# A graph network kernel: the gathers of the message stages in a POOL loop, their indices copied six at a time, and the sums of PE in a loop

## The chip, the cores and the metric

The kernel runs on one core of a Trainium2 chip. The metric is the device time of one execution in microseconds (us). The engines are TensorE (PE, its weight loads PEld), VectorE (DVE), ScalarE (ACT), GpSimd (POOL) and SyncE (SP); DMA engines move data between device memory and the on-chip memory (SBUF). Engines wait for each other with semaphores, all written out by hand.

## The reference

Four graph layers run over the same graph: 625 nodes of 768 features and 10000 edges (src, dst, a type of 8 and a type of 34), each on relu(layernorm(x)) and added to x. The layers that matter here are the relational ones. Cut to that:

```python
def _rgcn_conv(x, src, dst, etype, W, root, b):
    seg = dst * num_rel + etype
    sums = segment_sum(x[src], seg)
    cnt = segment_sum(ones, seg)
    mean = (sums / maximum(cnt, 1.0)).reshape(num_nodes, num_rel, -1)
    return einsum('nri,rio->no', mean, W) + x @ root + b
# layer 0: two of these (8 types, relu between); layer 1: one (34 types), then a GCN; layers 2 and 3: graph attention
```

## The kernel before

For a relational layer the kernel multiplies first and sums along the edges afterwards. PE makes h·W_r for every type r, each float32 product as three passes of high and low parts (line 1553), ACT takes the results out of PSUM, and SP stores them as the rows of a table `U` in device memory. Then comes a *message stage*, three in all: phase 0 and 1 for the two convolutions with 8 types, phase 2 for the one with 34.

The edges were sorted by groups of 128 destination nodes and cut into NT = 84 tiles of 128 edges. For each tile four things happen in a message stage:

- POOL issues an indirect DMA (`gathers`, line 473) that brings the tile's 128 rows of `U`, 393 KB, into one of GB = 6 buffers `gat`. Before it, it waits for `agg_pe`: tile t needs tile t-6 to have been summed.
- DVE makes the tile's one-hot matrix with the edge weights (line 944), four buffers deep, waiting for the same `agg_pe`.
- PE waits for the one-hot and the gather and runs two float32 matmuls of 512 and 256 columns (line 1461; four records in a trace), which add the tile to the sums of its group in PSUM; the second raises `agg_pe`. Which PSUM bank it is comes from a register: every six tiles PE loads a packed number `grp` (line 1423).
- Nothing else of weight runs then: ACT is idle, and SP's loads for the next phase wait for buffers.

So the order is a ring: gather, DMA, PE, release, gather, with six buffers in it. POOL's gathers and PE's tiles are written out 84 times each per phase; the row numbers of a gather are read straight from the table `ix[:, table, t]`. DVE's part is a loop of seven turns of twelve tiles (GU = 12).

Elsewhere POOL already works in loops: `kinv` (lines 478 to 484) and `lookup` copy six columns of `ix` into a small tile `ixb` at a register's offset (`indices`, line 464), wait for the copy with `pool_idx`, and use `ixb` in six indirect DMAs. `indices` counts the semaphore `pool_idx` by a number k of earlier whole tables. The instruction `pool.sem_inc(S["pool_nop"], 1)` carries the wait that stands before it, since a DMA whose wait needs a register has it in front of it.

Of the kernel before, what the change touches and what calls it, by code (L numbers as in the profile page):

```python
# [24 lines left out]
NP = NG * P  # L25
# [4 lines left out]
NT = 84  # L30
R0, R1 = 8, 34
# [7 lines left out]
GB = 6  # L39
MB = 4  # L40
GU = 2 * GB
# [5 lines left out]
def gnn_kernel(nc, a, out):  # L47
    ctx = ExitStack()
    with ctx:
        def sb(name, shape, dt=F32):  # L50
            return ctx.enter_context(nc.sbuf_tensor(name, shape, dt))

        def sem(name):
            return ctx.enter_context(nc.semaphore(name))
# [12 lines left out]
        gat = arena[:, 6528:6528 + GB * D].rearrange("p (b n) -> p b n", b=GB)  # L67
# [40 lines left out]
        def edge(shape, dt=F32):  # L108
# [39 lines left out]
        ix = sb("ix", [P, 4, NT], I32)  # L148
        ixb = sb("ixb", [P, GU], I32)
# [38 lines left out]
        U = nc.dram_tensor("U", [R1 * NP, D], F32, kind="Internal").ap()  # L188
# [8 lines left out]
        S = {n: sem(n) for n in (  # L197
            "x_in edges_in dve_nop w64_in consts vec_ok ln_var ln_std ln_h hT_tp hT_hi hT_lo "
            "w_hi w_lo steps evac pool_idx pool_nop msg_oh agg_pe acc_out "
            "srt_rs srt_ps srt_rhs srt_mm srt_tab cnt_oh cnt_pe k_inv kinv_st w_pr w_done "  # L200
            "key_ok key_tp ov_ok urow_st urow_ok u_zero l_oh l_pe l_ix h_st lix_ok hc_tp hc_hi hc_lo "
            "v_in v_hi v_lo v_mm v_ev "
            "c_oh c_pe ct_tp ct_cp deg_ok deg_sq gcn_y gcn_mm gcn_ev x_ok ln_c ln_cc ct_ln "
            "elu_v elu_m elu_e bd_z bd_tp bd_ok ft_mm ft_ev chain out_st").split()}
# [7 lines left out]
        g_in = [sem(f"g_in{b}") for b in range(GB)]  # L212
# [51 lines left out]
        def sums(c0, g=None):  # L264
            if g is None:
                return ps[:, 0:NG, :] if c0 == 0 else psf[:, 512 * NG:512 * NG + 256 * NG].rearrange("p (g n) -> p g n", g=NG)
            return psf[:, ds(512 * g, 512)] if c0 == 0 else psf[:, ds(512 * NG + 256 * g, 256)]
# [172 lines left out]
        def _(pool):  # L440
# [21 lines left out]
            def indices(table, it, j, k):  # L462

                pool.tensor_copy(ixb[:, j:j + GB], ix[:, table, ds(GU * it + j, GB)]).then_inc(S["pool_idx"], 1)  # L464
                pool.wait_ge(S["pool_idx"], NT // GB * k + 2 * it + j // GB + 1)
                pool.sem_inc(S["pool_nop"], 1)

            def gathers(phase):

                table = (0, 0, 3)[phase]  # L470
                for t in range(NT):
                    pool.wait_ge(S["agg_pe"], NT * phase + t + 1)
                    pool.indirect_dma_start(out=gat[:, t % GB, :], out_offset=None, in_=U[0:NP * (R0, R0, R1)[phase], :],  # L473
                                            in_offset=bass.IndirectOffsetOnAxis(ap=ix[:, table, t:t + 1], axis=0)).then_inc(g_in[t % GB], 16)

            pool.wait_ge(S["srt_tab"], 1)
            pool.wait_ge(S["kinv_st"], 16)
            with pool.Fori(0, NT // GU) as it:
                for j in range(GU):
                    if j % GB == 0:  # L480
# [3 lines left out]
                                            in_offset=bass.IndirectOffsetOnAxis(ap=ixb[:, j:j + 1], axis=0)).then_inc(k_in[j // GB], 16)  # L484
            pool.wait_ge(S["w_done"], NT // GB + 2)
            for g in range(NG):
                pool.wait_ge(u_st[g], 16 * (ST_C1 + 2 * R0))
            gathers(0)

            pool.wait_ge(S["urow_st"], 16)  # L490
            def urow_out(it, j):

                pool.wait_ge(k_in[j], 16 * GB * it + 16 * GB * (NT // GU + 1))
                pool.tensor_copy(ix[:, 3, ds(GU * it + GB * j, GB)], urow_g[:, GB * j:GB * (j + 1)]).then_inc(S["urow_ok"], 1)

            def lookup(it, first):
                for j in range(2):
                    indices(1, it, GB * j, 1)
                    if not (first and j == 0):
                        pool.wait_ge(S["urow_ok"], 2 * it + j - 1 + 1)  # L500
                        pool.sem_inc(S["pool_nop"], 1)
                    for k in range(GB * j, GB * (j + 1)):
                        pool.indirect_dma_start(out=urow_g[:, k:k + 1], out_offset=None, in_=urow_d,
                                                in_offset=bass.IndirectOffsetOnAxis(ap=ixb[:, k:k + 1], axis=0)).then_inc(k_in[j], 16)
                    if j == 1:
                        urow_out(it, 0)
                    elif not first:
                        urow_out(it - 1, 1)
            pool.sem_inc(S["urow_ok"], 1)
            lookup(0, True)  # L510
            with pool.Fori(1, NT // GU) as it:
                lookup(it, False)
# [3 lines left out]
            for g in range(NG):  # L516
                pool.wait_ge(u_st[g], 16 * (ST_C2 + 2 * R0))
            gathers(1)

            pool.wait_ge(S["l_ix"], 1)  # L520
            pool.wait_ge(S["h_st"], 16)
            pool.wait_ge(S["hT_tp"], 3 * KT)
            with pool.Fori(0, R1 // 2) as it:
                for j in range(2):
# [4 lines left out]
                    for g in range(TC):  # L529
                        pool.indirect_dma_start(out=src_rows[:, TC * j + g, :], out_offset=None, in_=h_d,  # L530
                                                in_offset=bass.IndirectOffsetOnAxis(ap=lixb[:, j, g:g + 1], axis=0)).then_inc(hc_in[j], 16)
# [11 lines left out]
            for j in range(2):  # L543
                pool.wait_ge(v_st[j], n_ov * 16 + 16)
                pool.sem_inc(S["pool_nop"], 1)
            gathers(2)


# [848 lines left out]
        def _(pe):  # L1397
# [22 lines left out]
            def group(it, stride, o):  # L1420

                if o % GB == 0:
                    packed[0] = pe.value_load(grp[0:1, ds(stride // GB * it + o // GB, 1)], min_val=0, max_val=8 ** GB - 1)
                return ((packed[0] >> (3 * (o % GB))) & 7).with_bounds(min_val=0, max_val=NG - 1)
# [4 lines left out]
            def clear(i, banks):  # L1429

                if i:
                    pe.wait_ge(S["acc_out"], i)
                else:
                    pe.wait_ge(S["k_inv"], 1)
                for b in banks:
                    pe.matmul(ps[:, b, :], z16[:, 0:P], z16[:], start=True, stop=True)
# [13 lines left out]
            def messages(ph, q, i):  # L1450

                pe.wait_ge(S["evac"], 5 * q + 2)
                clear(i, range(8))
                for it in range(NT // GU):
                    for o in range(GU):
                        b = o % MB
                        g = group(it, GU, o)
                        pe.wait_ge(S["msg_oh"], NT * ph + o + GU * it + 1)
                        pe.wait_ge(g_in[o % GB], 16 * (NT // GB * ph + 2 * it + o // GB + 1))
                        for c0, c1 in ((0, 512), (512, D)):  # L1460
                            ins = pe.matmul(sums(c0, g), onehot[:, b, :], gat[:, o % GB, c0:c1], start=False,  # L1461
                                            stop=True, skip_group_check=True)
                        ins.then_inc(S["agg_pe"], 1)
# [176 lines left out]
            pe.wait_ge(S["hT_lo"], KT)  # L1640
            phase(Q_C1, R0)
            messages(0, Q_C2, 0)
            pe.wait_ge(S["acc_out"], 1)
            transpose(1)
            pe.wait_ge(S["hT_lo"], 2 * KT)
            clear(1, range(2, 8))
            phase(Q_C2, R0, 18, c_side(0))
            pe.wait_ge(S["l_ix"], 1)
            messages(1, Q_L1, 2)
            pe.wait_ge(S["ln_h"], 2 * NG)  # L1650
            transpose(2)
            pe.wait_ge(S["hT_lo"], 3 * KT)
            clear(3, range(2, 2 + NG))
            relations(6, c_side(1))
            further()
            messages(2, Q_GCN, 4)
            pe.wait_ge(S["acc_out"], 5)

            for s in range(NG):
                if s >= 2:  # L1660
                    pe.wait_ge(S["ct_cp"], s - 1)
                b = 4 + 2 * (s % 2)
# [10 lines left out]
            for i in range(2 * NG):  # L1673
                j, cols = i // 2, slice((i % 2) * HALF, (i % 2 + 1) * HALF)
# [72 lines left out]
            for g in range(NG):  # L1747
                b = 4 + 2 * (g % 2)
# [47 lines left out]
```

## Time and profile before

| | us |
|---|---|
| median of 3 runs | 2478.19 (2472.67 to 2482.26) |
| the profiled execution | 2472.67, its span 2470.9 |
| the three message stages, first to last matmul (392.67 to 512.55, 918.77 to 1039.81, 1689.39 to 1816.84) | 119.9, 121.0, 127.5 |
| busy in the span: PE / DVE / ACT / POOL | 2081.0 / 1192.3 / 696.7 / 567.3 |
| granted TensorE clock, mean | 0.883 |

The page gives busy time by engine, then the chain of work that ended last, then the costliest groups of instructions with the idle time before them. A timeline row reads: start, duration, engine, line, operation, and in brackets the idle time of that engine before it and what ended it. "issue" means that nothing in the profile ended it.

### The profile page before, as it was taken

The page shows a single profiled execution, that of the slowest core. Times are in us where ns is not written, and L with a number is a line of the kernel's source. Part 1 is how long each engine was busy: PE and PEld are TensorE (multiplying, and loading weights), DVE is VectorE, ACT ScalarE, POOL GpSimd, SP SyncE. Part 2 cuts the span into 40 slices and gives each one's busy share as a digit, 9 for nine tenths or more (in the row PEclk, how much of TensorE's full clock was granted, in tenths as well). Part 3 has the DMA queues.
Part 4 walks back from the last instruction along what each step waited for, and adds up shares of the span by engine and source line. Part 5 has one row for each costly group of instructions (what it writes and reads, how often), then busy time and mean ns, then how long its engine had stood idle before and what let it go on. Part 6 is the DMA issues. An engine that isn't in the chain of part 4 may idle for free.

```text
span 2470.9 us, 34116 instructions
## 1 busy us (share of the span) xinstructions
PE 2081.0 (84%) x10546; PEld 1774.8 (72%) x10547; DVE 1192.3 (48%) x2113; ACT 696.7 (28%) x899; POOL 567.3 (23%) x586
## 2 busy tenths in 40 slices
PE   3999879989998799779999999967988666667885
PEld 3999776567788785479999989954565656537775
DVE  5741213243342362345555555442233689546995
ACT  1222210012222110024545444530020256113553
POOL 0001765610006736412222222104620000000000
PEclk9999999989999899989999999978999766775555
DMA  3456547834445238637887777757830022001221
GB/s 108 152 172 181 160 120 245 272 95 142 141 151 176 90 120 265 213 123 241 264 264 254 260 249 259 246 185 239 272 121 7 18 81 89 12 24 44 65 64 53
DMA packets 206670, 385.13 MB, mean 156 GB/s; under 512 B 19347, under 2 KB 174373, under 8 KB 206590
## 3 DMA queue, kind: packets, MB, share of 16 engines
q1 hardware_dynamic: 173934, 253.16, 31.5%
q0 software_dynamic: 31216, 128.89, 16.9%
q10 hardware_dynamic: 1440, 1.97, 0.2%
q8 instruction: 55, 0.90, 0.1%
q14 instruction: 25, 0.20, 0.0%
HBM read 295.56 MB, written 88.39 MB: 155 GB/s over the span
## 4 chain that ended last, share of the span: by engine, by line
PE 65%; DVE 15%; issue 8%; DMA 6%; ACT 2%; another core or an unknown queue 2%; DVEq 1%; POOL 0%; SPq 0%; ACTq 0%; POOLq 0%
PE ps L1553 41%; PE ps L1461 12%; DVE arena L1244 2%; DMA arena<-U,ix 2%; DMA arena<-in_L_gnn_W_rel 2%; DVE arena L1267 2%; PE ps L1566 2%; DVE arena L1275 1%; PE ps L1753 1%; PE ps L1679 1%; PE ps L1720 1%; PE ps L1447 1%; PE ps L1406 1%; PE ps L1445 1%
## 5 line engine op out<-in xcount | busy, mean ns | idle before, releaser
L1553 PE MATMUL ps<-w_hi,hT_hi 128*128 128x384 f32 x2172 | 772.0, 355 | 62.9 <-DVE hT_lo L991 20.1
L1553 PE MATMUL ps<-w_hi,hT_lo 128*128 128x384 f32 x2172 | 744.1, 343 | 0.7 <-issue 0.6
L1553 PE MATMUL ps<-w_lo,hT_hi 128*128 128x384 f32 x2172 | 743.8, 342 | 1.0 <-issue 1.0
L1553 PEld LDWEIGHTS ps<-w_hi,hT_hi 128*128 128x128 f32 x2172 | 423.1, 195 | 76.2 <-issue 33.6
L1553 PEld LDWEIGHTS ps<-w_lo,hT_hi 128*128 128x128 f32 x2172 | 422.5, 195 | 2.6 <-issue 2.2
L1553 PEld LDWEIGHTS ps<-w_hi,hT_lo 128*128 128x128 f32 x2172 | 420.9, 194 | 1.2 <-issue 1.1
L1461 PE MATMUL ps<-arena,onehot 128*128 128x512 f32 x1008 | 345.4, 496 | 27.6 <-DMA arena<-U,ix 12.7
L1461 PEld LDWEIGHTS ps<-arena,onehot 128*128 128x128 f32 x1008 | 186.5, 191 | 187.1 <-issue 177.0
L473 POOL DMA_INDIRECT arena<-U,ix x252 | 250.0, 992 | 193.3 <-PE ps L1461 85.7
L1720 PE MATMUL ps<-R,arena 128*128 (+2 forms) x1000 | 211.6, 394 | 62.4 <-ACT arena L732 62.1
L1720 PEld LDWEIGHTS ps<-R,arena 128*128 128x128 f32 x1000 | 202.0, 306 | 78.7 <-issue 75.9
L1019 DVE TENSOR_TENSOR w_lo<-arena,w_hi 128x2304 fp32r<-128x2304 f32 x67 | 171.5, 2560 | 144.3 <-ACT w_hi L615 140.5
L564 ACT ACTIVATE arena<-ps 128x384 f32<-128x384 f32 x160 | 78.3, 492 | 520.8 <-PE ps L1553 410.5
L944 DVE TENSOR_SCALAR onehot<-iota,tab,wgt 128x128 f32<-128x128 f32 x252 | 87.9, 365 | 268.8 <-PE ps L1461 200.8
L827 DVE TENSOR_TENSOR w_lo<-arena,w_hi 128x2304 fp32r<-128x2304 f32 x45 | 114.8, 2554 | 129.8 <-ACT w_hi L557 116.0
L615 ACT ACTIVATE w_hi<-arena 128x2304 fp32r<-128x2304 f32 x67 | 142.6, 2129 | 60.3 <-DMA arena<-in_L_gnn_W_rel 60.2
L526 POOL COPY lixb<-lidx 128x2 int32 x34 | 35.2, 1034 | 388.5 <-PE ps L1566 356.1
L620 ACT ACTIVATE arena<-ps 128x384 f32<-128x384 f32 x136 | 66.5, 489 | 199.9 <-PE ps L1553 186.5
L464 POOL COPY ixb<-ix 128x6 int32 (+1 forms) x28 | 10.5, 374 | 474.6 <-DMA urow_d<-counts 239.7
L1406 PE MATMUL ps<-ident,h 128*128 128x128 f32 x210 | 45.2, 388 | 85.7 <-DVE h L811 60.0
L991 DVE SCALAR_TENSOR_TENSOR hT_lo<-ps,hT_hi 128x512 fp32r<-128x512 f32 x102 | 70.1, 687 | 97.4 <-ACT hT_hi L597 97.4
L1406 PEld LDWEIGHTS ps<-ident,h 128*128 128x128 f32 x210 | 35.9, 201 | 94.7 <-DVE h L811 32.1
(226 smaller groups left out, 2161.5 us busy)
## 6 DMA issues: line engine op xcount, KB each, us to landing
arena<-in_L_gnn_W_rel SPq DMA_DIRECT2D x74, 1152.0 KB, 5.8
U<-arena SPq DMA_DIRECT2D x292, 192.0 KB
arena<-in_L_gnn_W SPq DMA_DIRECT2D x36, 1152.0 KB
U<-z SPq DMA_DIRECT2D x28, 864.0 KB
arena<-terms_d SPq DMA_DIRECT2D x42, 320.0 KB, 3.9
arena<-rows_d SPq DMA_DIRECT2D x21, 320.0 KB, 3.6
arena<-in_L_gnn_root SPq DMA_DIRECT2D x4, 1152.0 KB
arena<-U,ix POOLq DMA_INDIRECT x252
```

Of the source, the lines that this page charges most:

```text
L473: pool.indirect_dma_start(out=gat[:, t % GB, :], out_offset=None, in_=U[0:NP * (R0, R0, R1)[phase], :], in_offset=bass.IndirectOffsetOnAxi ...
L564: act.activation(dst, ps[:, (o + g) % 2, 0:HALF] if len(dst.shape) == 2 else ps[:, (o + g) % 2, 0:HALF].rearrange("p (h c) -> p h c", h=ds ...
L615: act.activation(w_hi[:, 1 - j], raw[:, 1 - j], cp).then_inc(S["w_hi"], 1)
L620: act.activation(ust[:, TC * j + g, :], ps[:, g, 0:HALF], cp).then_inc(S["evac"], 1)
L827: dve.tensor_tensor(w_lo[:, o % 2], raw[:, o % 2], w_hi[:, o % 2].bitcast(F32), ALU.subtract).then_inc(S["w_lo"], 1)
L944: dve.tensor_scalar(onehot[:, b, :], iota[:, 1:P + 1], tab[:, 1, ds(t, 1)], wgt[:, ph // 2, ds(t, 1)], ALU.is_equal, ALU.mult).then_inc(S[ ...
L991: dve.scalar_tensor_tensor(hc[j][1][:, 2 * i:2 * i + 2, :], ps[:, 7, :].rearrange("p (k n) -> p k n", k=2), 0.0, hc[j][0][:, 2 * i:2 * i + ...
L1019: dve.tensor_tensor(w_lo[:, 1 - j], raw[:, 1 - j], w_hi[:, 1 - j].bitcast(F32), ALU.subtract).then_inc(S["w_lo"], 1)
L1406: ins = pe.transpose(psf[:, 512 * b + P * g:512 * b + P * (g + 1)], h[:, g, P * kt:P * (kt + 1)], ident[:])
L1461: ins = pe.matmul(sums(c0, g), onehot[:, b, :], gat[:, o % GB, c0:c1], start=False, stop=True, skip_group_check=True)
L1553: ins = pe.matmul(acc, l, r[:, j, kt, :], start=(n == 0), stop=(n == 3 * KT - 1))
L1720: ins = pe.matmul(ps[:, 6 + j, (c + 1) * g:(c + 1) * (g + 1)], pt[:, b, P * g:P * (g + 1)], R[:, t, ds((2 * it + j) * (c + 1), c + 1)], st ...
```

## The change

POOL's 84 gathers of a phase become a loop of seven turns with twelve gathers. At the first of every six it calls `indices`, so it waits for `agg_pe`, copies six columns of the table to `ixb`, waits for the copy and then issues the DMA; at the other five the wait stands in a semaphore instruction in front of the DMA. PE's message loop turns from written-out code into a loop of seven turns with the same twelve tiles. The numbers k in `indices` move on by one, as there are more copies.

```diff
+            def gather(it, j, phase):
+
+                t = j + GU * it
+                b = j % GB
+                table = (0, 0, 3)[phase]
+                pool.wait_ge(S["agg_pe"], NT * phase + t + 1)
+                if b == 0:
+                    indices(table, it, j, (1, 3, 4)[phase])
+                else:
+                    pool.sem_inc(S["pool_nop"], 1)
+                pool.indirect_dma_start(out=gat[:, b, :], out_offset=None, in_=U[0:NP * (R0, R0, R1)[phase], :],
+                                        in_offset=bass.IndirectOffsetOnAxis(ap=ixb[:, j:j + 1], axis=0)).then_inc(g_in[b], 16)
+
             def gathers(phase):
-
-                table = (0, 0, 3)[phase]
-                for t in range(NT):
-                    pool.wait_ge(S["agg_pe"], NT * phase + t + 1)
-                    pool.indirect_dma_start(out=gat[:, t % GB, :], out_offset=None, in_=U[0:NP * (R0, R0, R1)[phase], :],
-                                            in_offset=bass.IndirectOffsetOnAxis(ap=ix[:, table, t:t + 1], axis=0)).then_inc(g_in[t % GB], 16)
+                with pool.Fori(0, NT // GU) as it:
+                    for j in range(GU):
+                        gather(it, j, phase)
...
-                    indices(1, it, GB * j, 1)
+                    indices(1, it, GB * j, 2)
...
                 clear(i, range(8))
-                for it in range(NT // GU):
+                with pe.Fori(0, NT // GU) as it:
                     for o in range(GU):
```

POOL's queue at phase 0, before; `agg_pe` is the release by PE:

```order
L473 DMA arena<-U,ix 128x768 [waits u_st3,u_st2,u_st4,u_st1,agg_pe,u_st0,w_done]
L473 DMA arena<-U,ix 128x768 [waits agg_pe] x83
```

The same place after the change, the first of seven turns down to the second copy (four of the six gathers' rows read alike):

```order
L482 ISA
L464 ISA [waits agg_pe]
L464 COPY ixb<-ix 128x6
L465 ISA
L478 DMA arena<-U,ixb 128x768 [waits pool_idx]
L473 REGISTER_ALU
L478 DMA arena<-U,ixb 128x768 [waits agg_pe]
...
L464 ISA [waits agg_pe]
L464 COPY ixb<-ix 128x6
L465 REGISTER_ALU
L478 DMA arena<-U,ixb 128x768 [waits pool_idx]
```

Each sixth gather now stands behind a copy that itself waits for PE's release, and each of the others has a register instruction in front.

PE's queue at the seventh tile of phase 0, before:

```order
L1423 TENSOR_LOAD grp
L1423 ISA x2
L1461 REGISTER_ALU [waits g_in0,msg_oh]
L1461 ISA
L1461 MATMUL ps<-arena,onehot 128x512
L1461 ISA
L1461 MATMUL ps<-arena,onehot 128x256
```

And after, the seventh tile and the end of a turn:

```order
L1434 ISA
L1434 TENSOR_LOAD grp
L1434 ISA x2
L1469 REGISTER_ALU
L1470 ISA [waits msg_oh]
L1472 REGISTER_ALU [waits g_in0]
L1472 ISA
L1472 MATMUL ps<-arena,onehot 128x512
L1472 ISA
L1472 MATMUL ps<-arena,onehot 128x256
...
L1465 REGISTER_ALU
L1465 COMPARE_AND_BRANCH
```

PE's matmuls are the same; in front of them the sequencer has one or two register instructions more per tile, one for the address of `grp`, and a branch per twelve tiles.

## Rows read from the trace of the kernel before

**Rows 1.** The page, chain that ended last; costliest groups (the last number: idle before, releaser).
```profile
PE ps L1553 41%; PE ps L1461 12%; DVE arena L1244 2%; DMA arena<-U,ix 2%; DMA arena<-in_L_gnn_W_rel 2%; DVE arena L1267 2%; PE ps L1566 2%; DVE arena L1275 1%; PE ps L1753 1%; PE ps L1679 1%; PE ps L1720 1%; PE ps L1447 1%; PE ps L1406 1%; PE ps L1445 1%
...
L1461 PE MATMUL ps<-arena,onehot 128*128 128x512 f32 x1008 | 345.4, 496 | 27.6 <-DMA arena<-U,ix 12.7
...
L473 POOL DMA_INDIRECT arena<-U,ix x252 | 250.0, 992 | 193.3 <-PE ps L1461 85.7
```

**Rows 2.** Busy time by engine in the three message stages.
```profile
core 0: us, PE busy (x) PEld busy (x) DVE busy (x) ACT busy (x) POOL busy (x), PEclk, DMA share, GB/s
392.60:512.60 120.00, 114.23 (x336) 61.64 (x336) 28.97 (x84) 0.00 (x0) 73.93 (x78) 1.00 0.78 256
918.70:1039.90 121.20, 113.66 (x336) 61.66 (x336) 28.93 (x84) 0.00 (x0) 74.08 (x78) 1.00 0.78 254
1689.30:1816.90 127.60, 117.50 (x336) 63.19 (x336) 28.51 (x84) 0.00 (x0) 77.42 (x82) 0.97 0.79 263
```

**Rows 3.** Timeline of POOL, first message stage: start us, us, instruction, idle before it.
```profile
394.50 0.94 POOL L473 DMA_INDIRECT arena<-U,ix  x1 [11.86 <-PE ps L1461]
395.79 0.94 POOL L473 DMA_INDIRECT arena<-U,ix  x1 [0.34 <-PE ps L1461]
...
406.08 0.94 POOL L473 DMA_INDIRECT arena<-U,ix  x1 [1.61 <-PE ps L1461]
...
442.49 0.95 POOL L473 DMA_INDIRECT arena<-U,ix  x1 [1.80 <-PE ps L1461]
443.74 0.95 POOL L473 DMA_INDIRECT arena<-U,ix  x1 [0.30 <-issue]
...
505.69 0.94 POOL L473 DMA_INDIRECT arena<-U,ix  x1 [1.36 <-PE ps L1461]
```

**Rows 4.** The same of the second and third stage.
```profile
920.60 0.95 POOL L473 DMA_INDIRECT arena<-U,ix  x1 [5.22 <-PE ps L1461]
...
1032.08 0.95 POOL L473 DMA_INDIRECT arena<-U,ix  x1 [0.30 <-issue]
...
1700.51 0.95 POOL L473 DMA_INDIRECT arena<-U,ix  x1 [4.54 <-PE ps L1461]
...
1808.48 0.95 POOL L473 DMA_INDIRECT arena<-U,ix  x1 [0.30 <-issue]
```

**Rows 5.** Timeline of DVE at the pause of 442 us.
```profile
442.41 1.07 DVE L944 TENSOR_SCALAR onehot<-iota,tab,wgt 128x128 f32<-128x128 f32 x3 [2.55 <-PE ps L1461]
```

**Rows 6.** Timeline of PE at the same place.
```profile
439.62 6.72 PE L1461 MATMUL ps<-arena,onehot 128*128 128x512 f32 x20
446.85 1.55 PE L1461 MATMUL ps<-arena,onehot 128*128 128x512 f32 x4 [0.51 <-issue]
448.78 5.42 PE L1461 MATMUL ps<-arena,onehot 128*128 128x512 f32 x16 [0.38 <-DMA arena<-U,ix]
```

**Rows 7.** Timeline of POOL in the loop that gathers the reciprocals.
```profile
302.87 0.97 POOL L483 DMA_INDIRECT counts<-kinv_d,ixb  x1 [0.79 <-issue]
...
309.15 0.95 POOL L483 DMA_INDIRECT counts<-kinv_d,ixb  x1 [0.30 <-issue]
310.09 0.21 POOL L464 COPY ixb<-ix 128x6 int32 x1
311.09 0.97 POOL L483 DMA_INDIRECT counts<-kinv_d,ixb  x1 [0.79 <-POOL ixb L464]
```

**Rows 8.** PE instructions of the loop head L1493 (PEldq: the sequencer): ns min/median/max.
```profile
L1493 PEldq COMPARE_BRANCH  x4: 76/208/212, 569.2 to 696.4; - x4
```

**Rows 9.** The load of the packed groups, L1423.
```profile
L1423 PEldq TENSOR_LOAD <-grp x84: 295/302/905, 161.6 to 1805.6; - x84
```

**Rows 10.** Queues in the first message stage: packets, MB, share.
```profile
q8 instruction: 5, 0.08, 0.3%
```

**Rows 11.** The same in a stretch where PE loops four times.
```profile
q8 instruction: 2, 0.03, 0.1%
```

**Rows 12.** Timeline of PE at the start of the third stage.
```profile
1697.32 2.92 PE L1461 MATMUL ps<-arena,onehot 128*128 128x512 f32 x4 [3.39 <-DMA arena<-U,ix]
```
## The prediction

> **What bounds the kernel now.** I read the page first. Its chain of waits [rows 1] is mostly PE at the weight products (L1553, 41%), which the change leaves alone. The lines that it touches are L1461, the sums of the message stages (12% of the chain), with gathers (arena<-U,ix) for 2% more, and L473, POOL's gathers. So only three stretches matter, 119.9, 121.0 and 127.5 us long, 368.4 together; what the change is worth is read there.
>
> The table by stretch [rows 2] shows PE busy for 114, 114 and 118 us of these: PE is the busiest, but not closed up. POOL is busy only about 74 us in each, which is misleading, because of the 0.30 us between any two gathers. The timeline of POOL gives the real price: 442.49 to 443.74, 1.25 us per gather back to back [rows 3]. PE takes 1.29 per tile while nothing holds it (POOL in step with PE, 394.50 to 395.79 [rows 3]). POOL can hence run only 3% faster than PE. The mean is neither: 77 gathers from 394.50 to 505.69 are 1.444 us each [rows 3], the second stage has 1.448 (77 from 920.60 to 1032.08), the third 1.440 (75 from 1700.51 to 1808.48) [rows 4]. I take 1.444.
>
> Where do the missing 0.15 us per tile go? I followed one pause. POOL sits idle for 1.80 us before its gather at 442.49 and names PE [rows 3]. DVE, which waits for the same semaphore, then starts three one-hots in a row at 442.41 [rows 5]. But PE shows an unbroken run of 20 matmuls from 439.62 to 446.34 [rows 6], five tiles, one end per 1.29 us. So the releases of three tiles arrived together and the oldest came about 2 x 1.29 = 2.6 us late. PE then pays: the gather of 442.49 feeds the tile that starts at 446.85 (4.36 us later), after 0.51 of idle time, and the next tile waits 0.38 more [rows 6]. The first stage has eleven POOL pauses above 1 us after its first gather, in nine places (two of them are double), from 406.08 with 1.61 to 505.69 with 1.36 [rows 3].
>
> The ring explains that. One turn of a buffer is gather to PE 4.36, the tile 1.55 [rows 6], release to gather about 0.3 (the reading of 394.50 to 395.79, where idle is 0.34 [rows 3]), so 6.2 us against six tiles at 1.29 = 7.74. It holds 1.5 us of lateness; 2.6 is 1.1 too much, near the 0.89 that PE is seen idle.
>
> The Trainium skill (Perfetto Trace Analysis, Tensor Engine Instruction) says that a matmul's end in a profile is estimated, and that the semaphore goes up only when PSUM has acknowledged the bytes. This trace agrees: three tiles released together beside evenly spaced ends. By it lateness belongs to PE's writes, and a slower POOL wouldn't cure it.
>
> **The change, part by part.**
>
> *The copy of six indices.* The trace has the new pattern already, in the loop for the reciprocals: last DMA of six at 309.15, copy at 310.09 for 0.21, then 0.79 idle, then the next DMA at 311.09. From 302.87 to 311.09 six DMAs take 8.22 us [rows 7] where six written out take 7.50. So POOL's floor becomes 8.22 / 6 = 1.37 per gather, above PE's 1.29: PE is no longer what sets the pace when nothing is late, POOL is. If nothing else counted, the copy would add 0.12 per gather to a POOL-bound stage. But the stage isn't bound by POOL now: its waits beyond 0.30 come to 111.19 - 77 x 1.25 = 14.9 us per stage, and 13 copies (the first is ahead of PE) add 13 x 0.72 = 9.4, less than that. So much of the cost falls in pauses.
>
> *The wait in front of the DMA.* Where the wait stood on the DMA itself, the DMA began 0.34 after its predecessor though it was waiting for PE [rows 3]. Now a semaphore instruction waits, and the DMA is handed over after it. The nearest rows are the 0.79 from the copy's end to the DMA, across just such an instruction [rows 7]. While POOL is behind, this overlaps the DMA before; only after a pause is it open, 0.79 - 0.3 = 0.5 us. Low bound zero.
>
> *The sum per gather.* Per pause, the new turn is 4.36 + 1.55 + 2.6 + (0.3 or 0.79) = 8.8 or 9.3 us against six gathers in 8.22: 0.6 or 1.1 us too long. Nine places per stage over 77 gathers make 0.070 or 0.129. So the mean becomes 1.37 + 0.07 = 1.44 or 1.37 + 0.13 = 1.50. The two ends are the whole spread of the dispatch cost; I take the middle, 1.47, since each group's first gather pays the copy and the others only the wait. That is +0.026 over 1.444, times 252 = +6.6 us.
>
> *PE's loop.* A taken branch is 0.208 us in PE's sequencer [rows 8], about 0.4 with the register instructions beside it by my estimate (twice the branch), and the load of `grp`, 0.302 [rows 9], gets an address instruction. At 21 turns the worst is 21 x 0.4 = 8.4 us. Most of it lies under the idle time of PE at a group's first tile, since POOL's copy falls in the same tile (8.22 - 7.74 = 0.48 per six). I count a third, +2.5. The saving in PE's code is nothing: five instruction blocks are fetched in the stage, 0.3% of the queues [rows 10].
>
> *The start of a stage.* In the first two, POOL has its first six gathers out 11.86 and 5.22 us before PE frees a buffer [rows 3, 4], so the first copy is hidden. In the third, PE stands 3.39 us for a gather at 1697.32 [rows 12]; the first copy moves that by the copy and its gap, 0.21 + 0.79 = +1.0.
>
> *`lookup` with another k*: the same instructions, 0.
>
> Sum: 6.6 + 2.5 + 1.0 = +10 us. Against the profiled execution, 2472.67, that is 2483; it is the fastest of three runs, 5.5 under the median, so on the median of 2478.19 I predict 2488.
>
> **The rivals.**
>
> *Nothing visible.* The copies fall entirely in POOL's pauses. For it: 14.9 us of pauses per stage against 9.4 of copies. Against: the pauses are not spread like the copies, and after each POOL is behind and runs back to back, where every 0.72 delays a tile. Gives 2478, within 3.
>
> *Faster, the lateness absorbed.* POOL's slower pace widens the ring from 7.74 to 8.22, so it holds 8.22 - 6.2 = 2.0 us of lateness instead of 1.5. If releases come less late when PE has small rests, and stay under 2.0, there are no stalls, and the mean is the floor, 1.37: (1.37 - 1.444) x 252 = -19, with the start -18: 2460. It decides at a lateness of 2.0 us; the one that I read is 2.6, which speaks against.
>
> *Much slower, nothing absorbed.* POOL pauses as long as today and the costs come on top: 0.12 for the copies and 9 x 0.5 / 77 = 0.06 for the waits, 0.18 x 252 = +45, 2523. For it: if each pause is set by lateness counted from POOL's own pace. Against: the ring's sum above.
>
> *Instruction fetches at each turn.* The Trainium skill (Runtime: NRT & Kernel Launch, Instruction fetch mechanics) warns that a taken branch out of the loaded window stalls for a fetch and that unrolled code is preferred. The trace shows no such thing for PE's loops: from 527 to 697 us, with four turns of a longer body, there are two blocks of instructions [rows 11], against five in the stage written out [rows 10], and the longest branch is 0.21 [rows 8]. As a mechanism of this kernel, a turn that waited for one transfer would lose up to what a gather takes to reach PE, 4.36: 21 x 4.36 = +92. I leave it 2%.
>
> **How the numbers follow.** Forecast (slower by 3 to 20 us) 0.55; nothing visible 0.20; lateness absorbed 0.10; nothing absorbed 0.13; fetches 0.02. A measurement of this kernel tells about 0.5%, 12.4 us, from no change. Of the forecast's 0.55, its own range is 2479 to 2500 and about half lies over 2490.6; with 0.15 from the slow rivals that makes slower 0.42. Faster is the absorbed case, 0.10. The rest, 0.48, is no change. The range leaves out the two far slow cases (0.15) and half of the fast one (0.05): 2467 to 2508.
>
> **What would show it.** In the changed profile: POOL's timeline with a copy before every sixth gather and 8.2 us from one to the next in undisturbed places; waits of POOL for PE shorter in total than the 14.9 us per stage above the gaps; mean of gathers 1.45 to 1.50; PE's idle time at L1461 over the 27.6 us of now [rows 1], named by the gather; all of the difference inside the three message stages. It would be wrong if the mean stays at 1.44 or falls towards 1.37 (lateness absorbed), if pauses of POOL keep their 1.2 to 1.9 us and the mean goes over 1.6, or if PE is idle at the loop's turns with nothing named.

## The result, and the profile after

The changed kernel takes 2498.1 us (median of five runs, 2491.17 to 2499.43) against 2481.14 for the kernel before, five runs beside it: ratio 1.008, 95% interval 1.0052 to 1.0108. It is 17 us slower, where 10 us were forecast: under 1%, but the interval leaves out 1. The profiled execution took 2495.63, its span 2493.9.

The page, the chain and the two groups, the lines that answer to [rows 1]:

```profile
PE ps L1564 38%; PE ps L1472 9%; DMA arena<-U,ixb 3%; DMA arena<-in_L_gnn_W_rel 3%; DVE arena L1255 2%; DVE arena L1278 2%; DVE arena L1286 1%; PE ps L1577 1%; PE ps L1764 1%; PE ps L1690 1%; PE ps L1731 1%; PE ps L1458 1%; PE ps L1456 1%; PE ps L1779 1%
...
L1472 PE MATMUL ps<-arena,onehot 128*128 128x512 f32 x1008 | 352.2, 499 | 40.7 <-issue 18.3
...
L478 POOL DMA_INDIRECT arena<-U,ixb x252 | 244.1, 969 | 136.1 <-issue 69.1
```

PE's idle time ahead of the message matmuls went from 27.6 to 40.7 us. POOL's ahead of its gathers fell from 193.3 to 136.1, but that isn't all less waiting: 53 us of the 193.3 were the three waits for a stage to begin, and these now stand ahead of a copy. What names PE fell from 85.7 us [rows 1] to 53.8 ahead of gathers and 18.0 ahead of copies, 71.8 in all. So POOL waits somewhat less, PE more. The three stages by engine, as [rows 2]:

```profile
core 0: us, PE busy (x) PEld busy (x) DVE busy (x) ACT busy (x) POOL busy (x), PEclk, DMA share, GB/s
393.45:521.10 127.65, 116.36 (x336) 60.47 (x336) 29.45 (x82) 0.00 (x0) 77.03 (x91) 1.00 0.75 240
935.85:1064.25 128.40, 115.70 (x336) 61.11 (x336) 28.75 (x82) 0.00 (x0) 76.86 (x91) 1.00 0.74 239
1709.20:1841.24 132.04, 120.16 (x336) 61.92 (x336) 28.43 (x82) 0.00 (x0) 79.98 (x95) 0.97 0.78 253
```

The stages are 7.7, 7.4 and 4.6 us longer, 19.7 together, at the same granted clock. The span is 23.0 longer; the other 3.3 are +0.8 ahead of the first stage, +8.5 between first and second, -4.6 between second and third and -1.4 behind, nearly all in code that the change leaves alone. So the difference is where the forecast had it, and the stages alone grew by twice its size. POOL's timeline in the first stage, as [rows 3]:

```profile
429.25 0.95 POOL L478 DMA_INDIRECT arena<-U,ixb  x1 [1.88 <-PE ps L1472]
431.82 0.96 POOL L478 DMA_INDIRECT arena<-U,ixb  x1 [1.62 <-PE ps L1472]
432.78 0.19 POOL L464 COPY ixb<-ix 128x6 int32 x1
433.80 0.97 POOL L478 DMA_INDIRECT arena<-U,ixb  x1 [0.83 <-issue]
435.08 0.95 POOL L478 DMA_INDIRECT arena<-U,ixb  x1 [0.31 <-issue]
...
440.09 0.95 POOL L478 DMA_INDIRECT arena<-U,ixb  x1 [0.30 <-issue]
441.04 0.20 POOL L464 COPY ixb<-ix 128x6 int32 x1
442.06 0.97 POOL L478 DMA_INDIRECT arena<-U,ixb  x1 [0.82 <-POOL ixb L464]
```

From 433.80 to 442.06 are six gathers and a copy in 8.26 us, the 8.22 of the forecast [rows 7]. But just before them, at 429.25 and 431.82, POOL sits through 1.88 and 1.62 us of waits for PE: the pauses are still there. The mean gather, from the ninth to the last of each stage, is 1.526, 1.547 and 1.550 us, against 1.448, 1.452 and 1.440 in the same measure before; 1.50 was the upper end of the forecast.

The queue of instruction fetches in the first stage, as [rows 10]:

```profile
q8 instruction: 1, 0.02, 0.1%
```

One block instead of five. That is all that the shorter program saves there.

### The profile page after: what moved, and what is told of

The parts are those of the page before. It is cut to its first block, busy times and chain, and to the rows that moved or that the text cites. A ratio compares the mean times of both kernels' runs of the same rounds, so it can differ in the third digit from the quotient of the medians.

```text
span 2493.9 us, 35129 instructions
## 1 busy us (share of the span) xinstructions
PE 2077.0 (83%) x10546; PEld 1758.0 (70%) x10547; DVE 1192.5 (48%) x2113; ACT 695.6 (28%) x899; POOL 574.5 (23%) x628
## 3 DMA queue, kind: packets, MB, share of 16 engines
q10 hardware_dynamic: 1440, 1.97, 0.2%
## 4 chain that ended last, share of the span: by engine, by line
PE 59%; DVE 15%; issue 10%; DMA 8%; another core or an unknown queue 3%; ACT 3%; POOL 1%; DVEq 1%; SPq 0%; POOLq 0%; ACTq 0%
PE ps L1564 38%; PE ps L1472 9%; DMA arena<-U,ixb 3%; DMA arena<-in_L_gnn_W_rel 3%; DVE arena L1255 2%; DVE arena L1278 2%; DVE arena L1286 1%; PE ps L1577 1%; PE ps L1764 1%; PE ps L1690 1%; PE ps L1731 1%; PE ps L1458 1%; PE ps L1456 1%; PE ps L1779 1%
## 5 line engine op out<-in xcount | busy, mean ns | idle before, releaser
L1472 PE MATMUL ps<-arena,onehot 128*128 128x512 f32 x1008 | 352.2, 499 | 40.7 <-issue 18.3
L478 POOL DMA_INDIRECT arena<-U,ixb x252 | 244.1, 969 | 136.1 <-issue 69.1
L464 POOL COPY ixb<-ix 128x6 int32 (+1 forms) x70 | 22.2, 317 | 555.9 <-DMA urow_d<-counts 238.2
L743 ACT ACTIVATE arena<-arena 128x640 f32<-128x640 f32 x100 | 73.4, 734 | 108.0 <-DVE arena L1286 93.2
```

The costliest lines, as they stand in the source:

```text
L478: pool.indirect_dma_start(out=gat[:, b, :], out_offset=None, in_=U[0:NP * (R0, R0, R1)[phase], :], in_offset=bass.IndirectOffsetOnAxis(ap= ...
L743: act.activation(out_tile(i % 2, i % NG), zt[:, i % NG, :], ACT.Exp).then_inc(s["p_ok"], 1)
```

## The experiments

Twelve runs were made, in three groups; each group had one chip and its own runs of the kernel before. These took 2481.9 us (29 runs) in the first, 2421.5 (17) in the second and 2419.4 (23) in the third: the chips differ by 60 us, and this turned out to be a clue. Ratios are to the kernel before of the same group, with 95% intervals. "Mean gather" is measured as above; "stages" is the sum of the three message stages of the one profiled execution. A cost in us in the text is a difference of medians; the ratio is worked out by itself and can differ from it by some us.

| kernel | median us | ratio | stages us | mean gather us |
|---|---|---|---|---|
| **first group** (before 2481.9) | | | | |
| before, profile shown ahead | | | 368.4 | 1.448 / 1.452 / 1.440 |
| PE's loop alone | 2482.31 | 0.9998 (0.9978 to 1.0017) | 366.9 | 1.452 / 1.456 / 1.446 |
| POOL's side alone | 2499.13 | 1.0071 (1.0049 to 1.0093) | 387.7 | 1.519 / 1.533 / 1.530 |
| copies alone | 2491.58 | 1.0052 (1.0032 to 1.0072) | 381.7 | 1.506 / 1.491 / 1.479 |
| wait apart alone | 2488.78 | 1.0039 (1.0017 to 1.0060) | 380.9 | 1.487 / 1.512 / 1.513 |
| **second group** (before 2421.5) | | | | |
| ring of five | 2447.65 | 1.0124 (1.0098 to 1.0150) | 363.6 | 1.425 / 1.377 / 1.387 |
| ring of seven | 2414.19 | 0.9966 (0.9951 to 0.9982) | 333.4 | 1.291 / 1.279 / 1.331 |
| POOL's side written out | 2447.42 | 1.0108 (1.0093 to 1.0123) | 366.0 | 1.407 / 1.405 / 1.468 |
| the same, ring of seven | 2437.66 | 1.0073 (1.0058 to 1.0089) | 357.1 | 1.383 / 1.379 / 1.442 |
| **third group** (before 2419.4) | | | | |
| before again | 2422.22, one run | | 339.7 | 1.297 / 1.320 / 1.295 |
| changed kernel again | 2442.37 | 1.0095 (1.0072 to 1.0118) | 360.4 | 1.391 / 1.402 / 1.412 |
| copies three gathers ahead | 2419.77 | 1.0000 (0.9981 to 1.0019) | 337.4 | 1.299 / 1.304 / 1.312 |
| ring of seven again | 2413.09 | 0.9977 (0.9965 to 0.9990) | 334.8 | 1.291 / 1.283 / 1.334 |

### First group: which part costs

**PE's loop alone.**

```diff
-                for it in range(NT // GU):
+                with pe.Fori(0, NT // GU) as it:
```

> The kernel before with PE's message loop alone turned into a loop of seven turns; POOL's gathers stay written out. Theory A (the sequencer of PE stands at a turn of the loop, as the changed kernel's trace shows it at 426 us: load of grp 0.69, assert 0.69, register instruction 0.70): PE is idle at the first tiles of six for some 10 us more than before in the three stages, and the time goes up by 6 to 12 us. Theory B (PE's loop is free, POOL's side carries the whole difference of 17 to 20 us): within 2 us of before.

Ratio 0.9998. The loop costs nothing that five rounds can tell, although each of its 21 turns has the branch (instructions of the loop head in this kernel, PEldq being PE's sequencer; ns min/median/max):

```profile
L1454 PEldq COMPARE_BRANCH  x21: 3/208/218, 404.2 to 1825.3; - x21
```

In this trace the first matmul behind a turn starts 1.16 us or more (median 1.28) after the end of the branch: PE's sequencer runs about one tile ahead of its matmuls, and 0.208 us of branch fits in.

**POOL's side alone**: the changed kernel with PE's tiles written out as before.

> The kernel before with POOL's side of the change alone (the loop, the copies of six indices, the wait in a semaphore instruction); PE's tiles stay written out. Theory A: 8 to 12 us slower than before, about half of the difference, with a mean of 1.48 us per gather. Theory B: 17 to 20 us slower, 1.53 us per gather. If the two halves hide behind each other, this run and the one with PE's loop add up to more than the difference.

Ratio 1.0071, +17.2 us, inside the interval of the whole change: POOL's side is the whole difference.

**Copies alone.** The 84 gathers stay written out, the wait stays on the DMA itself at five of six:

```diff
                     pool.wait_ge(S["agg_pe"], NT * phase + t + 1)
+                    if t % GB == 0:
+                        indices(table, t // GU, t % GU, (1, 3, 4)[phase])
...
-                                            in_offset=bass.IndirectOffsetOnAxis(ap=ix[:, table, t:t + 1], axis=0)).then_inc(g_in[t % GB], 16)
+                                            in_offset=bass.IndirectOffsetOnAxis(ap=ixb[:, t % GU:t % GU + 1], axis=0)).then_inc(g_in[t % GB], 16)
```

> POOL's gathers written out as before, but the indices copied six at a time as in the change; the wait for PE stays on the DMA itself at the other five. Shows the copy's cost alone: 13 copies per stage of 0.72 us. If the pauses of POOL take most of them in, +2 us in all; by the sum of my prediction's lower end (1.37 + 0.07 per gather) 0 to +2 as well; if nothing is absorbed, 0.12 x 252 = +28 us. I expect +6, less than the whole loop on POOL.

**Wait apart alone.** No copies, indices read from `ix` as before:

```diff
                     pool.wait_ge(S["agg_pe"], NT * phase + t + 1)
+                    pool.sem_inc(S["pool_nop"], 1)
                     pool.indirect_dma_start(...)
```

> POOL's gathers written out and reading the whole table, as before, but the wait for PE stands in a semaphore instruction in front of each DMA. Shows the cost of the hand-over after the wait alone. By my prediction 0.49 us per pause, in a ring of 7.74 us, nine places per stage: 27 x 0.49 = +13 us at most; zero if the sequencer hides it. I expect +6 to +10: a pause that begins with a gap of 0.79 instead of 0.3 us after PE's release, and the mean of a gather up from 1.44 to 1.47.

The copies cost +9.7 us (7.9 to 17.9 by the interval) where +6 was expected, the wait in its own instruction +6.9 (4.2 to 14.9), inside the +6 to +10 expected. Each alone is clear of 1, and 9.7 + 6.9 = 16.6 is close to the 17.2 of both together. How exactly they add up isn't shown: by the stages they are 13.3 and 12.5 against 19.3 for both, so they may hide behind each other by some us. (The profiled execution with the copies alone was the slowest of its twelve, 2510.20.) Nothing is left for POOL's loop either way.

On this chip the pauses took in more than half of the copies. From the seventh gather of a stage on, POOL's time beyond its own work (1.25 us a gather, 1.97 across a copy) was 14.9, 15.2 and 18.5 us per stage in the kernel before; with the copies alone it is 10.6, 9.5 and 12.1. That is 16.4 us less, of the 36 x 0.72 = 25.9 that the copies in this range take, and leaves 9.5. POOL's waits for PE in this kernel (us in total, times, longest; the second row is ahead of copies):

```profile
POOL arena L475 <- PE ps L1463: 32.7, 51, 3.8
...
POOL ixb L464 <- PE ps L1463: 29.0, 9, 13.4
```

They sum to 61.7 us, against 85.7 before [rows 1]. With the wait apart alone, POOL's time beyond its work grows instead, from 48.6 to 62.1 us in the three stages. What that wait does is seen in POOL's timeline of this second kernel:

```profile
397.15 0.95 POOL L474 DMA_INDIRECT arena<-U,ix  x1 [0.34 <-issue]
398.44 0.95 POOL L474 DMA_INDIRECT arena<-U,ix  x1 [0.34 <-issue]
399.73 0.95 POOL L474 DMA_INDIRECT arena<-U,ix  x1 [0.34 <-issue]
401.39 0.95 POOL L474 DMA_INDIRECT arena<-U,ix  x1 [0.71 <-issue]
```

While releases come in good time the semaphore instruction runs beside the DMA before it, and the step is still 1.29 us. When one is late, the idle time is charged to "issue" instead of PE: the wait was over in the sequencer, and the DMA had yet to be handed down. The semaphore instruction at 400.617 stands 0.777 us before the DMA of 401.394 (start to start, and the same at every gather above). Counted from the modelled end of the tile that frees the buffer to the start of the gather, the least in any stage is 0.27 us with the wait on the DMA and 0.81 with the wait apart.

### Second group: does the ring decide

The forecast stood on a ring of six buffers that holds 7.74 - 6.2 = 1.5 us of lateness. The size of the ring tests that. For a ring of GR buffers, tile numbers run on through the three phases:

```diff
-                    pool.indirect_dma_start(out=gat[:, t % GB, :], ...
+                    pool.indirect_dma_start(out=rows7[:, (NT * phase + t) % GR, :], ...
...
-                        pe.wait_ge(g_in[o % GB], 16 * (NT // GB * ph + 2 * it + o // GB + 1))
+                        T = NT * ph + GU * it + o
+                        pe.wait_ge(g_in[T % GR], 16 * (T // GR + 1))
...
-            pe.sem_inc(S["agg_pe"], GB)
+            pe.sem_inc(S["agg_pe"], GR)
```

**Five buffers.**

> The kernel before with five gather buffers in place of six (the same SBUF, the sixth part unused), POOL written out and reading its indices as before. Theory A (a turn of the ring of buffers decides): POOL may run only five gathers ahead of a release, five times 1.29 us are 6.45 us against a turn of 6.2 us, so only 0.25 us of a release's lateness stays hidden instead of 1.5 us. The mean gather rises from 1.45 us to between 1.55 and 1.80, 250 gathers: +25 to +90 us on the kernel before. Theory B (POOL's pauses are its own or the DMA queue's, whatever the releases do): mean gather 1.45 us as before, time within 5 us of the kernel before.

**Seven buffers.** The seventh lies in columns 5760 to 6527 of the arena, which the evacuations use between message stages.

> The kernel before with seven gather buffers (the seventh lies in the part of the SBUF that the evacuations use, idle in these stages), POOL written out and reading its indices as before. Theory A (turn of the ring): seven times 1.29 us are 9.03 us against a turn of 6.2 us, so 2.8 us of lateness are hidden, more than any seen (2.6 us). The mean gather falls to POOL's own 1.25 to 1.32 us: 30 to 48 us less than the kernel before. Theory B (pauses are POOL's or the queue's own): mean gather 1.45 us, within 5 us of the kernel before. Between them lies the case that VectorE's ring of four one-hot buffers takes over: mean 1.35 to 1.40, 12 to 25 us less.

Five buffers cost +26 us (ratio 1.0124), just inside the +25 to +90 expected; seven give 7 us back. So the number of buffers matters, which excludes the rival that POOL's pauses are its own. The sizes did not fit: at five the mean gather, 1.38 to 1.43, lies below the 1.55 expected, and at seven the gain is a quarter of the least expected. With seven, PE runs through the first stage without a stop:

```profile
389.19 108.62 PE L1464 MATMUL ps<-arena,onehot 128*128 128x512 f32 x336 [1.20 <-DVE onehot L946]
```

(PE's timeline of the ring of seven in its second run.) This is a whole message stage, 84 tiles, without one gap: 1.29 us per tile from end to end. The kernel before on the same chip has 109.4 us for that stage (the third group), so the gain was small because there were hardly any pauses to remove.

**POOL's side written out**, with six buffers and with seven: copies and separate waits as in the changed kernel, without the loop.

> The kernel before with everything that the change does on POOL except its loop: the six indices copied ahead of each sixth gather, and a semaphore instruction between wait and DMA at the others, all 84 gathers written out. PE is as before. Theory A (copy and wait cost the time, the loop none): +17 us on the kernel before, as POOL's side with its loop, 2498 to 2500, stages longer by some 19 us in sum. Theory B (the loop costs what the parts together leave over or more): the parts measured alone, 9.7 and 6.9 us, overlap in part, and this kernel is 5 us or more below the one with the loop.

> Seven gather buffers as in the run beside it, and on POOL the copy of six indices and the semaphore instructions of the change, written out. Theory A1 (with the turns out of the way POOL itself is the bound, so its own work counts in full): every sixth gather takes 1.97 us instead of 1.25, mean 1.38 us, so 0.12 us times 252 = 30 us slower than the ring of seven without them, about the time of the kernel before; the wait ahead of the DMA costs little there, since POOL seldom waits. Theory A2 (a longer ring hides copies too): within 8 us of the ring of seven without them. Theory B (pauses are POOL's own): 17 us above the ring of seven, and that one equal to the kernel before.

Written out, POOL's side costs 1.0108, +26 us where +17 was expected: the expectation was drawn from the first chip. With its loop, in the changed kernel of the third group, it is 1.0095. The intervals overlap, and POOL's loop costs nothing measurable either, though the two ran on different chips. With seven buffers the copies and waits still cost 23.5 us (2437.66 - 2414.19). That is theory A1, a little under its 30: a longer ring doesn't hide work that POOL does between two gathers.

### Third group: the kernel before on this chip, and the copies moved

**Before again.**

> The kernel before itself, profiled on the chip of this group, so that the stages of the three other kernels have their own measure. If the late releases of TensorE belong to the kernel, the mean gather is 1.44 to 1.45 us again and the three stages sum to 368 us; if they differ from chip to chip, as the ring of seven with its 7 us of gain where 30 were expected lets one think, the mean gather is 1.30 to 1.36 us on the chip whose kernel before takes 2421 us, and the stages sum to 337 to 345 us.

The mean gather is 1.30, the stages sum to 339.7 us instead of 368.4. DVE's timeline beside the place of [rows 5]:

```profile
439.81 0.35 DVE L944 TENSOR_SCALAR onehot<-iota,tab,wgt 128x128 f32<-128x128 f32 x1 [0.94 <-PE ps L1461]
441.10 0.35 DVE L944 TENSOR_SCALAR onehot<-iota,tab,wgt 128x128 f32<-128x128 f32 x1 [0.94 <-PE ps L1461]
442.39 0.35 DVE L944 TENSOR_SCALAR onehot<-iota,tab,wgt 128x128 f32<-128x128 f32 x1 [0.94 <-PE ps L1461]
```

One one-hot per 1.29 us: each release comes when its tile ends, where [rows 5] has three at once. Steps of over 1.9 us between two gathers, from the eighth gather on, number 1, 3 and 2 in the three stages here, against 11, 9 and 11 in the profile of before shown ahead. The late releases are mostly a matter of the chip, not of the kernel. The stages make 28.7 us of the difference of 60 between the chips; the rest lies outside them and wasn't followed.

**The changed kernel again.**

> The changed kernel, timed on the chip of this group. Theory A (POOL's copies and waits cost the time, the two loops nothing): the same ratio as POOL's side alone on a like chip, 1.007 where the kernel before takes 2480 us, and 1.011, as both written out, where it takes 2421 us. Theory B (the loops cost time by themselves): more than that by 0.003 or over.

+23.0 us, ratio 1.0095, with theory A's 1.011 in its interval, and its stages are 20.7 us over those of the kernel before. That is near the size on the first chip, but with almost no pauses to lose or fill, so it is made up in another way: there pauses took in much of the copies and the separate wait cost some of it back, here POOL's own work is the bound. POOL's timeline here:

```profile
444.90 0.19 POOL L464 COPY ixb<-ix 128x6 int32 x1
445.91 1.01 POOL L478 DMA_INDIRECT arena<-U,ixb  x1 [0.81 <-PE ps L1472]
447.23 0.96 POOL L478 DMA_INDIRECT arena<-U,ixb  x1 [0.30 <-PE ps L1472]
448.50 0.98 POOL L478 DMA_INDIRECT arena<-U,ixb  x1 [0.31 <-PE ps L1472]
...
452.29 0.94 POOL L478 DMA_INDIRECT arena<-U,ixb  x1 [0.30 <-issue]
453.23 0.20 POOL L464 COPY ixb<-ix 128x6 int32 x1
454.26 0.97 POOL L478 DMA_INDIRECT arena<-U,ixb  x1 [0.83 <-PE ps L1472]
```

454.26 - 445.91 = 8.35 us for six gathers, POOL back to back throughout (the two rows left out have 0.30 us of idle time each); the median step is 1.25 and 1.96 across a copy, 8.2 for six. PE needs 7.74 for six tiles, so POOL is behind by about 0.48 each time: 13 copies per stage, three stages, 0.48 x 39 = 18.7 us, where the stages show 20.7.

**Copies three gathers ahead.** The copies go to a tile `ixa` of three sets of six, so that a set isn't overwritten while an earlier gather may still read it; the wait for PE stays on each DMA.

```diff
+                    if t % GB == 3 and t + 3 < NT:
+                        n = (t + 3) % (3 * GB)
+                        pool.tensor_copy(ixa[:, n:n + GB], ix[:, table, t + 3:t + 3 + GB]).then_inc(S["pool_idx"], 1)
+                    if t % GB == 0:
+                        pool.wait_ge(S["pool_idx"], k + t // GB + 1)
+                        pool.sem_inc(S["pool_nop"], 1)
                     pool.wait_ge(S["agg_pe"], NT * phase + t + 1)
...
-                                            in_offset=bass.IndirectOffsetOnAxis(ap=ix[:, table, t:t + 1], axis=0)).then_inc(g_in[t % GB], 16)
+                                            in_offset=bass.IndirectOffsetOnAxis(ap=ixa[:, t % (3 * GB):t % (3 * GB) + 1], axis=0)).then_inc(g_in[t % GB], 16)
```

> The kernel before with the copies of six indices, but each issued three gathers ahead of its use, into a third set of six columns, so that the wait for the copy is met when POOL comes to it; the wait on TensorE stays on each DMA itself. All 84 gathers are written out. Theory A (what costs is that the copy and POOL's wait for it stand behind the release and in front of the gather, 0.72 us on every sixth turn): the copy itself of 0.2 us and its issue remain, 14 a stage, 0 to 10 us in all on the kernel before, under half of the 9.7 us of the copies in place. Theory B (POOL's time counts wherever the copy stands): +9 us or more, as with the copies in place.

Ratio 1.0000 (0.9981 to 1.0019), with the same 14 copies per stage. Its timeline of POOL:

```profile
405.37 0.95 POOL L484 DMA_INDIRECT arena<-U,ixa  x1 [0.35 <-PE ps L1472]
406.32 0.19 POOL L479 COPY ixa<-ix 128x6 int32<-128x6 int32 x1
406.68 0.97 POOL L484 DMA_INDIRECT arena<-U,ixa  x1 [0.16 <-issue]
407.96 0.95 POOL L484 DMA_INDIRECT arena<-U,ixa  x1 [0.30 <-PE ps L1472]
409.24 0.94 POOL L484 DMA_INDIRECT arena<-U,ixa  x1 [0.34 <-PE ps L1472]
410.53 0.94 POOL L484 DMA_INDIRECT arena<-U,ixa  x1 [0.35 <-PE ps L1472]
411.82 0.94 POOL L484 DMA_INDIRECT arena<-U,ixa  x1 [0.35 <-PE ps L1472]
413.11 0.94 POOL L484 DMA_INDIRECT arena<-U,ixa  x1 [0.35 <-PE ps L1472]
414.06 0.19 POOL L479 COPY ixa<-ix 128x6 int32<-128x6 int32 x1
414.42 0.97 POOL L484 DMA_INDIRECT arena<-U,ixa  x1 [0.16 <-issue]
```

The copy starts in the gap that POOL has between any two gathers, and only 0.16 us follows it instead of 0.81: the step with the copy in it is 1.31 us, and six take 414.42 - 406.68 = 7.74, PE's pace. So what costs isn't the copy but POOL's wait for it just in front of the gather, 0.8 us in which the next DMA isn't handed down. This rests on the timelines: on this chip no run has the copies in place without the separate waits, so the 23.0 us of the changed kernel aren't divided between the two.

**Ring of seven again.**

> The kernel before with seven gather buffers in place of six, once more, beside a profile of the kernel before on the same chip. Theory A (the ring hides lateness of releases): the mean gather is 1.28 to 1.33 us whatever that of the kernel before, so the gain is 250 times the difference of the two means: 29 us (2452) on a chip where the kernel before has 1.45, some 7 us (2414) on one where it has 1.32. Theory B (the gain is 7 us on any chip): 7 us also where the kernel before has 1.45.

6.3 us faster, with the kernel before at a mean gather of 1.30. The run doesn't decide between the theories. The mean gather of 1.28 to 1.33 is as A had it, but A's formula for the gain, 250 times a difference of 1.304 - 1.303, gives nothing here, while the stages are 4.9 us shorter; B has 7 us on any chip. The 29 us that A promises on a chip with late releases weren't seen, since no such chip came up again. It is the only version that beats both kernels, by 0.2 to 0.3%.

## Why the forecast was too small

The 17 us lie inside the forecast's own case (slower by 3 to 20 us; the prediction also writes that case as 2479 to 2500 where it would be 2481 to 2498) and inside the range. How close the centre came is in part luck: one term was far too small and another was for a cost that isn't there. The chances put no change (0.48) ahead of slower (0.42), which the measurement doesn't bear out.

*What bounds the stage.* Right on the first chip, and incomplete. I read POOL's pauses as a property of the kernel; before again has almost none. On such a chip PE's pace of 1.29 us is all that bounds a stage.

*The copy of six indices.* The price, 0.72 us and 8.22 for six, is what both profiles after show. "So much of the cost falls in pauses" held too: with the copies alone, 16.4 of 25.9 us did. What failed is the size of what is left. In *The sum per gather* the lower end, 1.37 + 0.07 = 1.44, is the kernel with copies and no cost of the wait, and it equals the 1.444 of before, a cost of nothing. That kernel was measured at 1.492 and +9.7 us. The 0.07 for stalls was too small, and this was visible beforehand: put into the same formula, the kernel before has a turn of 4.36 + 1.55 + 2.6 + 0.3 = 8.8 against 7.74, nine times in 77 gathers, which gives 1.29 + 0.12 = 1.41 where 1.444 was read. I didn't make that test. The formula is short by 0.03 to 0.05 per gather in both.

*The wait in front of the DMA.* Bounded by 0 and 0.5 us per pause, with the middle taken. By the time alone the middle was good: +6.9 us, where it stands for 0.03 x 252 = 7.6. By the profiles it is nearer to the upper end: 0.27 against 0.81 us from release to gather, and a mean gather of 1.504, 0.057 over the kernel before, where the spread of this term was 0.129 - 0.070 = 0.059. The interval, 4.2 to 14.9 us, holds both.

*The two together.* The changed kernel's mean is 1.541 in place of 1.47: +0.094 per gather instead of +0.026. The top of the forecast's spread, 1.50, is within 0.04 of it, which is what the formula also misses in the kernel before. POOL's time beyond its own work is 12.1, 13.7 and 15.5 us per stage, so it gave up 7.3 of the 25.9 that 36 copies cost, less than the 16.4 with the copies alone: the separate waits, which alone made the pauses 13.5 us longer, are in it too. The other 18.6 is most of the 19.7 by which the stages grew.

*PE's loop.* Forecast +2.5, measured 0 (2482.31 against 2481.9). In the changed kernel PE stands at one turn or another; its timeline:

```profile
424.78 2.31 PE L1472 MATMUL ps<-arena,onehot 128*128 128x512 f32 x7
428.57 6.71 PE L1472 MATMUL ps<-arena,onehot 128*128 128x512 f32 x20 [1.48 <-issue]
```

1.48 us with nothing named, at a turn, is one of the signs that I had named for being wrong, and the largest part of PE's idle time names nothing (18.3 of 40.7) where I had expected the gather. The run with the loop alone shows that the loop isn't the cause of a loss: in its three stages PE idles 0.47, 0.28 and 1.5 us at the turns, and the time is unchanged. The trace has three instructions of PE's sequencer of 0.69 us each ahead of that matmul, the load of `grp` among them, which takes 0.302 as a rule [rows 9]. Such slow ones (0.5 to 1 us) number 37 in the stages of the changed kernel, 18 with the wait apart alone, whose tiles are written out, and none on the other two chips, in the same changed kernel either. Why they are there is open.

*The start of the third stage.* The copy stands there, 1703.26 to the gather at 1704.29, 1.03 us as forecast:

```profile
1703.26 0.19 POOL L464 COPY ixb<-ix 128x6 int32 x1 [21.02 <-DMA U<-arena]
1704.29 0.97 POOL L478 DMA_INDIRECT arena<-U,ixb  x1 [0.84 <-POOL ixb L464]
```

Whether it moved the end can't be told: the stretch around it varies by more from one profile to the next.

*The rivals.* Nothing visible and lateness absorbed are out as totals. Nothing absorbed, +45, is out on the first chip, where the pauses took in more than half of the copies. It also counted the copies at 0.12 against POOL's own pace and forgot the 0.04 per gather that POOL is quicker than PE. Instruction fetches at turns are out for PE (ratio 0.9998) and for POOL (with and without its loop alike). The Trainium skill (Runtime: NRT & Kernel Launch, Instruction fetch mechanics) warns of branches out of the loaded window; with one block fetched in a stage of seven turns that case didn't arise, and no run here tests it.

## What to carry to other kernels

Don't count on another engine's random pauses to pay for steady work: here they took in more than half of it on one chip and were hardly there on another. Compare the pace of the two engines, the new one with all its fixed gaps. A producer 3% quicker than its consumer has 0.24 us to spare in six steps, and a wait of an engine for its own small instruction can cost several times that instruction (0.8 us behind a copy of 0.2); issue it a few steps ahead and it is free. When a cost lies between two bounds, apply the formula first to the kernel before, whose answer is known.

## What was not expected of the hardware

- A semaphore instruction that carries the wait for the DMA behind it delays that DMA by half a microsecond on POOL when the release comes late: at least 0.81 us from the release to the DMA, where a wait on the DMA itself has 0.27.
- The same kernel takes 2481.9 us on one chip and 2419.4 to 2421.5 on two others, at the same mean granted clock (0.883). 28.7 us of it lie in the message stages, where releases by PE arrive late on the first chip. Why they do there is open.
- A taken branch takes 0.208 us in PE's sequencer and 0.045 in POOL's (medians, kernel before), and one in twelve tiles costs PE nothing (ratio 0.9998).
